# A graph layer and a routed feed-forward layer on one core: earlier fills, earlier sums, and buffers of 2 + 3 in place of 3 + 2

## What is computed

```python
h = item_feat @ W_item.T + b_item                 # 10000 x 128
b = layernorm(x) @ W_user.T + b_user
x = x + relu(adj @ h + b)                         # adj: 10000 x 10000, float32
xf = layernorm(x)
probs = softmax(xf @ gate_w + gate_b)             # 8 experts
top2_vals, top2_idx = top_k(probs, 2)
cw = zeros(N, 8) with top2_vals at top2_idx
for e in range(8):
    out += cw[:, e] * (gelu(xf @ W1[e] + b1[e]) @ W2[e] + b2[e])   # 128 -> 256 -> 128
x = x + out
```

## Time and profile before

| | |
|---|---|
| median of 3 runs | 1490.46 us (1488.32 to 1493.43) |
| the profiled execution | 1491.99 us |
| its span in the trace | 1490.2 us |
| PE busy | 1436.9 us, 96% |
| DVE busy | 1261.7 us, 85% |
| ACT busy | 1094.9 us, 73% |
| POOL busy | 713.4 us, 48% |
| DMA | 489.44 MB, mean 328 GB/s |
| L931 on DVE, 520 times | 884.3 us, mean 1718 ns |
| L717 on ACT, 520 times | 749.6 us, mean 1454 ns |

### The profile page before, as it was taken

How to read it: one execution, slowest core, us unless ns; L and a number is a source line. 1 busy time by engine, 2 the same in 40 slices (tenths; PEclk the granted TensorE clock), 3 DMA queues, 4 the chain that set the end, 5 groups by cost and what they waited for, 6 DMA issues and landing times.

```text
span 1490.2 us, 20458 instructions
## 1 busy us (share of the span) xinstructions
PE 1436.9 (96%) x6682; PEld 1170.6 (79%) x6682; DVE 1261.7 (85%) x1775; ACT 1094.9 (73%) x1165; POOL 713.4 (48%) x397
## 2 busy tenths in 40 slices
PE   7999999999999999999997999999999999999998
PEld 6887787887877878887875788888887777777777
DVE  4888889889889889888896789898888987778797
ACT  4777767767767767777674878787877777778676
POOL 0005244334433442452442276867676784666631
PEclk9999999999999999999999999999999999999999
DMA  9999999999999999999998899999998988877348
GB/s 340 343 324 386 364 392 369 370 386 354 374 385 354 374 383 357 380 372 369 379 342 324 323 334 320 355 318 344 318 325 311 320 307 326 297 263 261 110 106 179
DMA packets 127335, 489.44 MB, mean 328 GB/s; under 512 B 26456, under 2 KB 32216, under 8 KB 126142
## 3 DMA queue, kind: packets, MB, share of 16 engines
q1 hardware_dynamic: 115422, 457.43, 84.2%
q0 software_dynamic: 11808, 30.71, 6.9%
HBM read 456.00 MB, written 40.99 MB: 334 GB/s over the span
## 4 chain that ended last, share of the span: by engine, by line
PE 63%; DVE 13%; ACT 9%; issue 7%; POOL 3%; DMA 2%; SPq 2%; ACTq 0%; DVEq 0%; POOLq 0%
PE p_agg L476 16%; PE p_agg L471 15%; PE p_agg L472 15%; DVE s_a_lo L931 7%; ACT s_a_hi L717 4%; POOL zs L1346 2%; ACT s_xtok L733 2%; PE p_hid L564 2%; PE p_hid L566 2%; PE p_hid L565 2%; ACT s_rows L762 1%; POOL rr L1355 1%; PE p_y L580 1%; PE p_hid L453 1%; PE p_y L581 1%
## 5 line engine op out<-in xcount | busy, mean ns | idle before, releaser
L931 DVE TENSOR_TENSOR s_a_lo<-s_raw,s_a_hi 128x1500 fp32r<-128x1500 f32 x520 | 884.3, 1718 | 108.2 <-PE p_agg L476 70.6
L717 ACT ACTIVATE s_a_hi<-s_raw 128x1500 fp32r<-128x1500 f32 x520 | 749.6, 1454 | 203.3 <-PE p_agg L476 189.2
L471 PE MATMUL p_agg<-s_a_hi,s_h_hi 128*128 128x500 f32 x1560 | 626.9, 402 | 4.1 <-ACT s_a_hi L717 4.1
L472 PE MATMUL p_agg<-s_a_hi,s_h_lo 128*128 128x500 f32 x1560 | 607.8, 390 | 0.0
L476 PE MATMUL p_agg<-s_a_lo,s_h_hi 128*128 128x500 f32 x1560 | 447.1, 395 | 13.8 <-DVE s_a_lo L931 11.5
L476 PEld LDWEIGHTS p_agg<-s_a_lo,s_h_hi 128*128 128x128 f32 x1560 | 287.6, 189 | 98.1 <-DVE s_a_lo L931 43.3
L1355 POOL DMA_INDIRECT rr<-s_ysb,s_dests x192 | 278.9, 1453 | 175.0 <-DVE s_ysb L1170 125.5
L471 PEld LDWEIGHTS p_agg<-s_a_hi,s_h_hi 128*128 128x128 f32 x1560 | 295.0, 189 | 63.9 <-ACT s_a_hi L717 6.2
L472 PEld LDWEIGHTS p_agg<-s_a_hi,s_h_lo 128*128 128x128 f32 x1560 | 295.2, 189 | 57.4 <-issue 3.2
L1346 POOL DMA_INDIRECT zs<-s_rows,s_idx x136 | 233.1, 1714 | 205.5 <-DVE s_idx L1089 157.3
L1322 POOL TENSOR_TENSOR s_gt<-s_ebase,s_gt 125x32 f32<-125x32 f32 x20 | 127.8, 6390 | 89.5 <-DVE s_gt L1015 86.0
(11 more groups left out here) (215 smaller groups left out, 1292.7 us busy)
## 6 DMA issues: line engine op xcount, KB each, us to landing
s_raw<-adj SPq DMA_DIRECT2D x520, 750.0 KB, 6.5
s_wraw<-w SPq DMA_DIRECT2D x56, 256.0 KB
s_zt<-zs SPq DMA_DIRECT2D x48, 264.0 KB, 3.7
out_s<-rr POOLq DMA_DIRECT2D x12, 512.0 KB, 10.3
s_xtok<-x_tok SPq DMA_DIRECT2D x20, 256.0 KB, 6.7
s_xt<-x_t SPq DMA_DIRECT2D x20, 250.0 KB, 6.3
zs<-s_early SPq DMA_DIRECT2D x18, 264.0 KB, 5.5
out_s<-s_x1s SPq DMA_DIRECT2D x17, 256.0 KB, 6.0
```

The costliest lines, as they stand in the source:

```text
L471: mm(o, h_hi[:, k * D:(k + 1) * D], hi, start=(k == 0), stop=False)
L472: mm(o, h_lo[:, k * D:(k + 1) * D], hi, start=False, stop=False)
L717: fn(a_hi[:, n % HIS, :], raw[:, n % RAW, :], ACT.Copy).then_inc(hi_made, 1)
L931: tt(a_lo[:, n % LOS, :], raw[:, n % RAW, :], a_hi[:, n % HIS, :].bitcast(F32), ALU.subtract)\
```

## The change

`HIS` and `LOS` are exchanged: two buffers of rounded chunks and three of remainders. Together they are five as before. The fills of a group are moved six chunks up (to chunks 336 and 466), and no longer wait for the group's scattered rows, only for the first entry of the table (`tab_made >= 2 g + 1`). The first tiles' loads stay at their chunks (346 and 476, now named `FIRST_ZT`), and the waits for scattered rows and the table stand with them. The additions of blocks 0 to 11 are moved from POOL's end to behind the last six tiles' sends: rank 0 behind tiles 42 to 44, rank 1 behind tiles 45 to 47; the rank 1 additions of blocks 0 to 11 wait for the six of rank 0 alone.

```diff
--- before.py
+++ after.py
@@ -21,7 +21,7 @@
 KC = 3
 CH = KT // KC
 NCH = BLOCKS * CH
-RAW, HIS, LOS = 6, 3, 2
+RAW, HIS, LOS = 6, 2, 3
 TAILP = 96
 EPS = 1e-5
 FEAT = 2
@@ -65,8 +65,9 @@
 XR = 8
 
 
-FILL_AT = [(hi + 1) * CH + 4 for lo, hi in GROUPS]
-FIRST_W1 = [at + E // 2 + 1 for at in FILL_AT]
+FILL_AT = [(hi + 1) * CH - 2 for lo, hi in GROUPS]
+FIRST_ZT = [(hi + 1) * CH + 8 for lo, hi in GROUPS]
+FIRST_W1 = [at + 1 for at in FIRST_ZT]
 STEP = [(FIRST_W1[1] - FIRST_W1[0]) / NTG[0], (NCH - 2 - FIRST_W1[1]) / NTG[1]]
 W1_AT = [FIRST_W1[g] + int(STEP[g] * i) for g in range(2) for i in range(NTG[g])]
 NI = NT + ND
@@ -76,7 +77,7 @@
 ZT_AT = [w - 3 for w in W1_AT[:NT]]
 SPLIT_AT = [w - (1 if o < NT else 2) for o, w in enumerate(W1_AT)]
 W_LOAD = [0, 0] + [w + 5 for w in W1_AT[:NT - 2]] + [NCH - 3, NCH - 2]
-ZT_LOAD = [0, 0] + [max(W1_AT[k - 2] + 5, FILL_AT[k >= NTG[0]] + E // 2) for k in range(2, NT)]
+ZT_LOAD = [0, 0] + [max(W1_AT[k - 2] + 5, FIRST_ZT[k >= NTG[0]]) for k in range(2, NT)]
 LAST = NCH + ND + 5
 
 
@@ -323,6 +324,9 @@
                     sp.wait_ge(w_split, o - 1)
                 else:
                     sp.wait_ge(h_prod, CH + 1)
+                    sp.wait_ge(tab_made, 2)
+                if o == NTG[0]:
+                    sp.wait_ge(tab_made, 4)
                 if BIAS <= o < NT:
                     sp.wait_ge(gelu_done, o - BIAS + 1)
                     sp.wait_ge(yt_made, o - BIAS + 1)
@@ -338,10 +342,12 @@
                     sp.wait_ge(turned, k - 1)
                     sp.wait_ge(ext_made, 2 * (k - 1))
                 if k == 0:
-                    sp.wait_ge(filled, 16 * E)
                     sp.wait_ge(spare_filled, 16 * 2)
-                if k == NTG[0]:
-                    sp.wait_ge(filled, 2 * 16 * E)
+                if k in (0, NTG[0]):
+                    g_ = int(k > 0)
+                    sp.wait_ge(tab_made, 2 * (g_ + 1))
+                    sp.wait_ge(scattered, 2 * 16 * SUBS * GROUPS[g_][1])
+                    sp.wait_ge(filled, 16 * E * (g_ + 1))
                 r = sp.value_load(tab[0:1, 0, k:k + 1], min_val=0, max_val=ZROWS - T)
                 sp.dma_start(zt[:, k % 2, :, :].rearrange("p s w -> p (s w)"),
                              zs[bass.ds(r, T), :].rearrange("(p s) w -> p (s w)", s=SUBS))\
@@ -353,8 +359,7 @@
 
             def fill_end(g, e):
                 if e == 0:
-                    sp.wait_ge(scattered, 2 * 16 * SUBS * GROUPS[g][1])
-                    sp.wait_ge(tab_made, 2 * (g + 1))
+                    sp.wait_ge(tab_made, 2 * g + 1)
                 r = sp.value_load(fillat[0:1, g, e:e + 1], min_val=0, max_val=SPARE0[g] - T)
                 sp.dma_start(zs[bass.ds(r, T), :].rearrange("(p s) w -> p (s w)", s=SUBS),
                              fill.rearrange("p s w -> p (s w)")).then_inc(filled, 16)
@@ -411,7 +416,7 @@
                     if 0 <= n - FILL_AT[g_] < E // 2:
                         fill_end(g_, 2 * (n - FILL_AT[g_]))
                         fill_end(g_, 2 * (n - FILL_AT[g_]) + 1)
-                if n == FILL_AT[0] + E // 2:
+                if n == FIRST_ZT[0]:
                     load_w(0)
                     load_w(1)
                     for k in range(2):
@@ -1331,7 +1336,7 @@
                     for j in range(2):
                         pool.wait_ge(sent[j], 16 * SUBS * tiles_of(j, NTG[0] if i < PAIRS else NT))
                 else:
-                    pool.wait_ge(rank0_added, 16 * (PAIRS + 1))
+                    pool.wait_ge(rank0_added, 16 * (PAIRS + (i == PAIRS)))
                 rows_of = slice(first * T, last * T), slice(k * RANK + first * T, k * RANK + last * T)
                 out, new = (t[rows, :].rearrange("(p s) d -> p (s d)", p=P) for t, rows in zip((out_s, rr), rows_of))
                 gp.dma_start(out, new, max_dma_last_dim=8192, accum_op=ALU.add).then_inc((rank0_added, rank1_added)[k], 16)
@@ -1391,11 +1396,17 @@
                 for k in range(NT):
                     if YOUT_AT[k] == n:
                         send(k)
+                        i = k - (NT - PAIRS)
+                        if 0 <= i < PAIRS // 2:
+                            add_rank(2 * i, 0)
+                            add_rank(2 * i + 1, 0)
+                        elif i >= PAIRS // 2:
+                            add_rank(2 * i - PAIRS, 1)
+                            add_rank(2 * i - PAIRS + 1, 1)
             power_of_rs(BLOCKS)
             power(BLOCKS - 1)
-            for k in range(2):
-                for i in range(PAIRS + 1):
-                    add_rank(i, k)
+            add_rank(PAIRS, 0)
+            add_rank(PAIRS, 1)
 
 
 def kernel(**inputs):
```

## The result

Median of 4 runs 1554.07 us (1553.85 to 1555.14), against 1491.71 for the kernel before on the same chip: 1.0419 times its time, 95% interval 1.0402 to 1.0436. The change makes the kernel 4.2% slower. The profiled execution took 1555.14 us, 1553.3 of it in the span. (In the code of after, L717, L931, L471, L472 and L476 of before have become L722, L936, L476, L477 and L481.)

The account below looks back on a forecast made before the run. PE's own row of instructions was taken to set the pace, 2.04 us a plain chunk. 57.6 + 8.4 - 16.5 + 1 + 1 + 1 = +52.5 us on 1491.99 gave 1544.5, so a median of 1543 (1517 to 1572).

Parts of the forecast that it names:

- The likeliest case: Plain chunks: two rounded buffers close a loop of 4.30 us per two chunks, against PE's 4.07; chance 0.76.
- The exchange, 57.6 + 8.4: Two rounded buffers cost 57.6 us in blocks 1 to 12 and 8.4 in blocks 13 to 19.
- the model's 58.1: Step-by-step starts of one 26-chunk block with three rounded buffers: 58.1 us, against 57.9 in the trace.
- the quarter of the gaps: Blocks 13 to 19: one gap in four is bare, so a quarter of 4.8, 1.2 us a block.
- The fills, -16.5 + 1 + 1: First tiles of both groups: SP's stop goes, -16.5 us; 1 comes back for the tile's load, 1 for DMA.
- the term for the crowded DMA: Where the moved fills land: eight fills, 2.1 MB, in a full DMA stretch cost 1 us, bounds 0 and 4.
- The additions, +1: Last tiles: moved additions run beside the tiles' loads and cost 1 us, bounds 0 and 10.
- Hidden: Rival, plain chunks: the loop is shorter than PE's 4.07 us, so the exchange costs nothing, 1476 us; chance 0.05.
- the stop only moves: Rival, first tiles: the tile's load still meets an unfinished scatter, 12 of 16.5 us stay, 1555; chance 0.06.
- The loop costs clock: Rival, blocks 1 to 12: waits at c = 5 also halve the clock, 2.2 us each, 26 in all, 1569; chance 0.07.
- Tiles in full: Rival, blocks 13 to 19: the exchange costs 34 us there in place of 8.4, 1569; chance 0.06.
- ACT's idle time was to be ended by PE: Sign of being right: before ACT's rounding, PE ends the idle time in nearly all 520 chunks.

Follow-up runs that it names:

- e1: The kernel before with only the buffers exchanged, 2 rounded and 3 remainder, fills and additions where they were: 1557.50 us, 1.0445.
- e3: The changed kernel with 3 rounded and 2 remainder buffers and all additions back at POOL's end, so only the fills are moved: 1480.28 us, 0.9922.
- e2: The changed kernel with 3 rounded and 2 remainder buffers, so only fills and additions are moved: 1484.26 us, 0.9948.
- e5: The changed kernel, but a rounded chunk's buffer is released behind PE's six matmuls that read it and DVE's remainder: 1512.38 us, 1.0145.

## Why the prediction was right, and where it was off

The forecast was 1543 us (1517 to 1572) and slower; measured were 1554.07. The likeliest case, a closed loop of PE, ACT and DVE, is what happened.

- *The exchange, 57.6 + 8.4 = 66.0.* Measured alone +66.6. The loop is 4.32 us (forecast 4.30). The excess over PE's own work in blocks 1 to 11 of after is 1.3 at c = 5, 0.5 and 0.4 at 8 and 9, 0.7 at 10, 0.2 at 12, 0.5, 0.4 and 0.6 at 13 to 15, and 0.10 to 0.15 at each of twelve others (4, 6, 7, 11 and 18 to 25), 1.5 together: 6.1, piece by piece within 0.2 of what was written down. The 0.4 and 0.6 at 14 and 15 were there before the change. The 2.5 us missing in blocks 1 to 12 are the model's 58.1 for before, where the trace has 57.94, and some 0.6 us in block 12. In the tile blocks 14 to 17 and 19 the quarter of the gaps gave +6.0 for five blocks, and +6.0 was measured, but not evenly: 1.1, 2.7, 0.6, 1.6 and 0.1. The sum was right, the even share was not. And blocks 13 and 18, forecast at 2.4, came to -3.9 and +1.8 in e1, since the first tiles' stops shrank. So seven blocks took 3.8 us in place of 8.4; in the traces of e1 and before the exchange is 64.0 us, and that the medians met the sum to 0.6 is in part luck.
- *The fills, -16.5 + 1 + 1.* Alone they gave -10.6. The stops behind SP did go, as forecast: 12.2 us at c = 5 to 8 of block 13 (the 1.3 at c = 5 that e3 still pays is counted in the 4.2 below), and PE's wait for the tile is 0.3 us in after. What failed is the term for the crowded DMA, 1 us, which measured 4.2 in block 13 of e3 and some 2.8 in after (1.5 at c = 1, 1.7 at c = 9 less the 0.4 of other blocks). I had taken 1 of at most 4 us because the slower loop asks 8% less of DMA and six chunks are prefetched; but with the share at 1.01 the prefetch is used up in a few chunks, and a later landing reaches ACT. The bytes of the fills, 5.7 us at full rate, were the better guide. And at c = 12 after pays 3.1 us, before 2.1: the first Gelu, told below, where a lead that the exchange has taken away had hidden a part.
- *The additions, +1.* Measured +4.0 (e2 less e3), +4.1 in the last stretch of after. I looked for the price in POOL's row, where there is none, and took the DMA share of the last tiles, 0.67; the adds of rank 1 fall behind those, beside the loads of weights that ACT waits for. This is what the Trainium skill says (DMA: Bandwidth & Descriptors, Issuing engines are not separate DMA queues), and the trace agrees: DMAs issued by POOL made ACT wait 4.57 us for one issued by SP.
- *The parts together.* -10.6, +4.0 and +66.6 make 60.0, and 62.4 was measured. The excess of 2.4 has its likeliest place in block 13: part of what the fills remove the exchange had removed already, so that moving them takes away 2.2 us there (e1 83.4, after 81.2) and not 7.5 (before 87.3, e3 79.8). Those 5.3 us are more than the 2.4; what stands against the rest was not found.
- *Rivals.* "Hidden" fell with e1, "the stop only moves" with SP's rows in after. "The loop costs clock" fell as well: no stretch of blocks 1 to 12 has a granted clock below 1.00, with 1.3 us of waiting in each block at c = 5. "Tiles in full" fell: blocks 13 to 19 of e1 are 3.8 us longer than before's, not 34.
- *Signs that were wrong.* ACT's idle time was to be ended by PE in nearly all 520 chunks; it was in 358. Behind a piece of its own ACT comes late and doesn't wait. And PE was to be idle for DVE at 5 us a block; in 560 to 732, 2.7 blocks, the table of waits has 4.1 us, 1.5 a block, since PE's rows cover the rest. The other signs held: no wait of DVE for PE worth the name, blocks at 62.9, the last store (issued at 1550.79, the third of SP's stores of `out_d`) ending the span. The lower end of the range, 1517, is not what its own terms give (1490.5 + 35 - 16.5 + 3 = 1512); nothing hung on it.
- *Two buffers.* The rule of the Trainium skill to double-buffer (Trainium Kernel Development and Optimization, Best Practices), read as "two do", would have had the exchange free. The runs disagree with that reading, by 66.6 us with a late release; with an early one (e5) two buffers still cost 20.8 us over before, fills and additions included.

The 11 us by which the median lies above the forecast are, by the table: blocks 1 to 12 2.5, block 13 2.9, the last stretch 3.1, block 18 1.0, block 0 1.0 (blocks 14 to 17 and 19 cancel). Block 0 varies from 90.6 to 92.6 between the traces of the kernels here, so its part is no effect of the change.

## What to carry to other kernels

A ring of buffers is too small when the time from its release round to its next full use (here PE's last matmul, ACT, DVE, PE's next remainder: 4.32 us) is longer than the work of that many turns (2 x 2.04), and the busy shares don't show it: ACT and DVE had slack. So look for the buffer whose release comes last before a spare is moved away from it, and release it with its last reader, which gave back 42 us of after and 4 to 5 of the version with three, at no memory. And a DMA that is moved must be costed in the stretch where it lands, by what that stretch has free and who waits for the next load there, not by who issues it.

## What the runs showed of the hardware

In after PE waits 2.54 us at the first Gelu, where ACT has a scaling, the loading of its table (1.28 us), Gelu, a rounding of its result and only then the chunk's rounding in one row, and PE then runs for a stretch at about half the clock (timelines of ACT and of PE, then the window):

```profile
881.93 1.28 ACT L805 ACT_TABLE_LOAD   x1
883.23 1.26 ACT L805 ACTIVATE s_g<-p_hid,s_bias 128x512 f32<-128x512 f32 x2
884.52 1.06 ACT L812 ACTIVATE s_gh<-s_g 128x1024 fp32r<-128x1024 f32 x1
885.49 1.44 ACT L722 ACTIVATE s_a_hi<-s_raw 128x1500 fp32r<-128x1500 f32 x1
```
```profile
886.98 0.50 PE L476 MATMUL p_agg<-s_a_hi,s_h_hi 128*128 128x500 f32 x1 [2.54 <-ACT s_a_hi L722]
```
```profile
889.00:892.40 3.40, 3.40 (x9) 2.73 (x10) 3.35 (x9) 1.73 (x2) 0.00 (x0) 0.55 0.68 235
```

A granted clock of 0.55 in a window means 1.2 GHz for nearly all of it, in place of 2.4; 3.4 us of it cost about 1.7 us. I had read the 0.50 of the earlier trace rows as belonging to the wait for the tile alone. Before has a second such stretch of 3.4 us, from 834 on, behind the same Gelu, where PE had waited only 1.53 us. In blocks 1 to 12 of after PE waits up to 1.1 us at one place and for less at many others, and the clock stays at 1.00. What sets the two apart, no run here tells.

A group of remainder matmuls that had to wait takes 0.96 us, one that had not 0.86, in the rows of after above. The starts say the same: behind a wait the second matmul starts 0.33 us after the first, else 0.24. The wait costs 0.1 us beyond itself.
